# A graph layer on one core: one turn's rows fetched by SP, a longer reach for the gathers, early statistics moved into the turns

## The reference

```
h   = relu(layernorm(x))                          # nodes
xn  = silu(h @ aw1 + ab1) @ aw2 + ab2             # the table, one row per node
W   = silu(edge_attr @ fw1 + fb1) @ fw2 + fb2     # filters, one row per edge, 50 inputs
agg = segment_sum(W * xn[src], dst)               # message of each edge, summed by node
out = x + h + silu(agg @ ow1 + ob1) @ ow2 + ob2
```

## Time and profile before

| | us |
|---|---|
| runs | 2394.49, 2394.53, 2397.10 (median 2394.53) |
| profiled execution, its own time | 2395.59 |
| its span in the trace | 2393.7 |
| PE busy / VectorE busy / ACT busy / POOL busy | 1300.2 / 1178.2 / 520.4 / 1525.4 |
| mean granted clock of TensorE | 0.74 of full speed |

### The profile page before, as it was taken

One profiled execution on the slowest core, in us unless ns is written; L12 is line 12 of the kernel. 1 busy time (PEld: TensorE's weight loads), 2 busy tenths in 40 slices (PEclk: granted clock), 3 DMA queues, 4 the chain that ended last, 5 costly groups with the idle time before them and its releaser, 6 DMA issues.

```text
span 2393.7 us, 13107 instructions
## 1 busy us (share of the span) xinstructions
PE 1300.2 (54%) x4526; PEld 701.8 (29%) x4526; DVE 1178.2 (49%) x1404; ACT 520.4 (22%) x545; POOL 1525.4 (64%) x1619
## 2 busy tenths in 40 slices
PE   2425665656554655566556555655655454555545
PEld 1313332323332333233223222323332232232323
DVE  3635454545554554555535544644454453554545
ACT  2312222212221222222222211211222121121211
POOL 7246666666666666666666666666666666666664
PEclk8667776778777677777668777876778686776776
DMA  4312122212212222212212212212212212212211
GB/s 140 143 30 79 45 80 81 75 54 84 82 51 81 53 75 79 81 47 82 86 45 83 80 46 88 79 50 84 83 51 80 81 50 81 80 51 85 56 46 37
DMA packets 62292, 171.46 MB, mean 72 GB/s; under 512 B 27088, under 2 KB 29648, under 8 KB 59024
## 3 DMA queue, kind: packets, MB, share of 16 engines
q0 software_dynamic: 51584, 105.75, 17.1%
q1 hardware_dynamic: 8192, 61.32, 6.8%
q10 hardware_dynamic: 2448, 3.54, 0.4%
HBM read 164.08 MB, written 6.42 MB: 71 GB/s over the span
## 4 chain that ended last, share of the span: by engine, by line
another core or an unknown queue 40%; PE 27%; ACT 15%; issue 14%; DVE 3%; DMA 0%; ACTq 0%; SPq 0%; DVEq 0%
PE banks L872 15%; ACT hid L435 7%; PE banks L864 7%; ACT hid L441 7%; PE banks L879 3%; PE banks L887 1%; PE banks L811 1%; ACT hs L455 1%; DVE stats L643 0%; ACT mid L464 0%; DVE stats L544 0%; PE banks L806 0%; PE banks L818 0%; DMA xs<-in_x 0%
## 5 line engine op out<-in xcount | busy, mean ns | idle before, releaser
L369 POOL DMA_INDIRECT xg<-node_table,src x1564 | 1478.6, 945 | 828.3 <-issue 453.2
L872 PE MATMUL banks<-hid,wts 128*128 128x512 f32 x806 | 535.3, 799 | 565.4 <-ACT hid L435 436.6
L672 DVE TENSOR_TENSOR banks<-banks,xg 128x1024 f32<-128x1024 f32 (+1 forms) x198 | 241.0, 1217 | 1090.2 <-remote 899.2
L864 PE MATMUL banks<-attr,wts 50*128 50x512 f32 x806 | 293.9, 810 | 444.8 <-issue 250.4
L675 DVE TENSOR_REDUCE sums<-banks 128x128 f32<-128x1024 f32 (+1 forms) x408 | 493.9, 1211 | 13.6
L441 ACT ACTIVATE hid<-banks,cols 128x1024 f32<-128x1024 f32 x202 | 224.5, 1111 | 914.0 <-remote 425.7
L435 ACT ACTIVATE hid<-banks,cols 128x1024 f32<-128x1024 f32 x202 | 224.4, 1111 | 825.0 <-remote 595.9
L872 PEld LDWEIGHTS banks<-hid,wts 128*128 128x128 f32 x806 | 179.9, 248 | 755.3 <-ACT hid L435 467.6
L879 PEld LDWEIGHTS banks<-ident,hid 128*128 128x128 f32 x1612 | 225.5, 171 | 204.2 <-issue 198.2
L879 PE MATMUL banks<-ident,hid 128*128 128x128 f32 x1612 | 284.5, 333 | 0.0
L679 DVE TENSOR_TENSOR banks<-banks,other 128x1024 f32<-128x1024 f32 (+1 forms) x204 | 248.7, 1219 | 7.0
(11 more groups left out here) (89 smaller groups left out, 279.5 us busy)
## 6 DMA issues: line engine op xcount, KB each, us to landing
attr<-in_attr SPq DMA_DIRECT2D x25, 2048.0 KB
xg<-node_table,src POOLq DMA_INDIRECT x1564, 2.5
out<-res ACTq DMA_DIRECT2D x8, 256.0 KB
xs<-in_x SPq DMA_DIRECT2D x3, 512.0 KB, 6.0
node_table<-res SPq DMA_DIRECT2D x3, 512.0 KB, 2.8
out<-res ACTq DMA_DIRECT2D x5, 192.0 KB
spare<-in_dst SPq DMA_DIRECT2D x1, 808.0 KB
src<-in_src SPq DMA_DIRECT2D x1, 808.0 KB
```

Of the source, the lines that this page charges most:

```text
L369: pool.indirect_dma_start(xg[:, i % XG, j, :], None, table[:, :], bass.IndirectOffsetOnAxis(ap=src[:, s * L + j:s * L + j + 1], axis=0))\
L672: dve.tensor_tensor(to, to, rows_of, ALU.mult).then_inc(signal, 1)
L864: i = pe.matmul(hid_ps[:, GC * half:GC * half + GC], fw1_s[at, :], attr[at, cols_of], start=True, stop=True)
L872: i = pe.matmul(hid_ps[:, at], w["fw2_s"][:, :], hid[:, s % 2, at], start=True, stop=True)
```

## The change

1. **Early gathers of x wait.** POOL's early gathers for pairs 2, 3, 4 and 5 wait for progress of the node stage (s_tr of chunk 0, then s_res of chunks 0, 1 and 3).
2. **Statistics move into the turns.** bn_stats for early pair r is done by VectorE in turn r + 1, the moments in turn 7, the square root (ACT) in turn 8, the scales in turn 9. Early tasks begin at turn 10, and the early turns become 30, 50, 72, 92, 114 and 136.
3. **fb2** is split only in the slow branch; its scratch now lies in hT.
4. **One turn by SP.** Turn 190 is not gathered by POOL. SP reads each of its 1,024 indices into a register and issues one 512-byte DMA from the table for it, 47 rows after each attr transfer, from turn 8 on, over 22 parts. VectorE waits for four new semaphores in turn 190.
5. **Reach.** POOL waits for fil_done of turn s - 3 instead of s - 2.
6. **Who waits for the gather.** PE waits for it ahead of the transposes, and VectorE no longer does (except in the last two turns). PE's pair sums come ahead of the transposes instead of after the filters, again except in the last two turns.
7. **One-hots** are built per turn with two instructions, in six buffers, instead of per two turns with three.
8. At the end ACT's last "middle" task comes ahead of the "stored" tasks that are left.

```
@@ constants
-BATCH = 2
-OH_SETS = 3
+OH_SETS = 6
-EARLY_TURNS = (20, 40, 64, 84, 108, 128)
-MAIN_TURNS = [s for s in range(PAIRS) if s not in EARLY_TURNS]
+EARLY_TURNS = (30, 50, 72, 92, 114, 136)
+SINGLE_TURN = 190
+MAIN_TURNS = [s for s in range(PAIRS) if s not in EARLY_TURNS and s != SINGLE_TURN]
+SINGLE_PARTS = SINGLE_TURN // PART - 1
+SINGLE_ROWS = -(-PC // SINGLE_PARTS)
+REACH = XG - LAG
+STAT_TURNS = tuple(range(1, EARLY_PAIRS + 1))
+VAR_TURN, STD_TURN, SCALE_TURN, EARLY_FROM = 7, 8, 9, 10
@@ SP
+            def fetch(r):
+                p, j = r // L, r % L
+                t = SINGLE_TURN * L + j
+                node = sp.value_load(src[p:p + 1, t:t + 1], min_val=0, max_val=NODE_TILES * P - 1)
+                sp.dma_start(x_single[p:p + 1, j, :], table[bass.ds(node, 1), :]).then_inc(fetched[r % 4], 16)
             for s in range(PAIRS):
                 pair(s)
+                if s % PART == 0 and s // PART in range(1, SINGLE_PARTS + 1):
+                    if s == PART:
+                        sp.wait_ge(src_in, 16)
+                        sp.wait_ge(s_tab, 16 * (AHEAD + table_writes(N_CHUNKS - 1)))
+                    first = (s // PART - 1) * SINGLE_ROWS
+                    for r in range(first, min(first + SINGLE_ROWS, PC)):
+                        fetch(r)
@@ POOL
+            table_at = {2: (s_tr, 0), 3: (s_res, 0), 4: (s_res, 1), 5: (s_res, 3)}
             for t in range(EARLY_PAIRS * L):
+                if t % L == 0 and t // L in table_at:
+                    signal, c = table_at[t // L]
+                    pool.wait_ge(signal, run(c))
...
-                    pool.wait_ge(fil_done, run(s - 2))
+                    pool.wait_ge(fil_done, run(s - REACH))
@@ ACT
-            act.wait_ge(s_var, 3)
-            act.activation(e_moments[:, 2, :], e_moments[:, 2, :], ACT.Sqrt).then_inc(s_std, 1)
...
+                if s == STD_TURN:
+                    act.wait_ge(s_var, 3)
+                    act.activation(e_moments[:, 2, :], e_moments[:, 2, :], ACT.Sqrt).then_inc(s_std, 1)
@@ VectorE, ahead of the turns (the eight fb2 steps go to the slow branch)
-            for t in range(EARLY_PAIRS * L):
-                if t % L == 0:
-                    dve.wait_ge(e_gathered[t // L], 16 * L)
-                i = dve.bn_stats(stats[:, t, :], e_x[:, t, :])
-            i.then_inc(s_step, 1)
-            step[0] += 1
-            dve.wait_ge(s_step, step[0])
-            moments_of(stats[:, 0:EARLY_PAIRS * L, :], e_moments)
-            scales_of(e_moments, 3)
+            def early_stats(r):
+                dve.wait_ge(e_gathered[r], 16 * L)
+                for t in range(r * L, (r + 1) * L):
+                    i = dve.bn_stats(stats[:, t, :], e_x[:, t, :])
...
@@ VectorE, one-hots
+            def one_hots(s):
+                nodes, to = iota[:, 0:WIN], onehot[:, s % OH_SETS, :, :]
+                dve.tensor_scalar(to[:, 0, :], nodes, ends[:, 0, s:s + 1], None, ALU.is_equal).then_inc(oh_done, 1)
+                dve.wait_ge(oh_done, 2 * s + 1)
+                dve.scalar_tensor_tensor(out=to[:, 1, :], in0=nodes, scalar=ends[:, 1, s:s + 1], in1=to[:, 0, :],
+                                         op0=ALU.is_equal, op1=ALU.subtract).then_inc(oh_done, 1)
@@ VectorE, pair
+                elif s == SINGLE_TURN:
+                    rows_of = x_single[:, :, :]
+                    for signal in fetched:
+                        dve.wait_ge(signal, 16 * PC // len(fetched))
                 else:
                     i = MAIN_OF[s]
                     rows_of = xg[:, i % XG, :, :]
-                    dve.wait_ge(gathered[i % XG], (i // XG + 1) * 16 * L)
...
+                if s in STAT_TURNS:
+                    early_stats(STAT_TURNS.index(s))
+                elif s == VAR_TURN:
+                    dve.wait_ge(s_step, step[0])
+                    moments_of(stats[:, 0:EARLY_PAIRS * L, :], e_moments)
+                elif s == SCALE_TURN:
+                    scales_of(e_moments, 3)
@@ PE, pair
                 pe.wait_ge(red_done, run(s, LAG))
+                if s not in HALVED:
+                    for a in SUMS_AT.get(s, ()):
+                        pair_sums(a)
+                if s in MAIN_OF and s not in HALVED:
+                    pe.wait_ge(gathered[MAIN_OF[s] % XG], (MAIN_OF[s] // XG + 1) * 16 * L)
                 by_edge(s)
                 if s + 1 < PAIRS:
                     filters(s + 1)
-                for a in SUMS_AT.get(s, ()):
-                    pair_sums(a)
+                if s in HALVED:
+                    for a in SUMS_AT.get(s, ()):
+                        pair_sums(a)
```

More of the change, by code:

```diff
@@ L107, in tasks @@
 def tasks():
-    done, free, outs, halves = [], 0, list(range(len(OUTS) - 1)), list(range(2 * EARLY_PAIRS))
+    done, free, outs, halves = [], EARLY_FROM, list(range(len(OUTS) - 1)), list(range(2 * EARLY_PAIRS))
     for s in range(PAIRS):
@@ L279, in gnn_layer @@
         half_gathered = [sem(f"half_gathered{i}") for i in range(2 * len(HALVED))]
+        fetched = [sem(f"fetched{i}") for i in range(4)]
         e_gathered = [sem(f"e_gathered{r}") for r in range(EARLY_PAIRS)]
@@ L452, in task @@
                         act.wait_ge(n_tr, n - 1)
+                    if n == 0:
+                        act.wait_ge(s_rstd, 3)
                     for j in range(TPG):
@@ L473, in _ @@
             act.wait_ge(s_left, 1)
-            act.wait_ge(s_rstd, 3)
             turns(pair, task)
+            task("out", "middle", len(TASKS), len(OUTS) - 1)
             for left in STEPS.get(PAIRS, ()):
                 task(*left)
-            for step in ("middle", "stored"):
-                task("out", step, len(TASKS), len(OUTS) - 1)
+            task("out", "stored", len(TASKS), len(OUTS) - 1)
             n = edges_left(act)
@@ L654, in _ @@
             dve.wait_ge(s_tab, 16 * (AHEAD + table_writes(N_CHUNKS - 1)))
-            def one_hots(k):
-                first, n = k * BATCH, min(BATCH, PAIRS - k * BATCH)
-                nodes = iota[:, 0:WIN].rearrange("p (o w) -> p o w", o=1).to_broadcast([P, n, WIN])
-                for m in range(2):
-                    of_row = ends[:, m, first:first + n].rearrange("p (n o) -> p n o", o=1).to_broadcast([P, n, WIN])
-                    dve.tensor_tensor(onehot[:, k % OH_SETS, 0:n, m, :], nodes, of_row, ALU.is_equal).then_inc(oh_done, 1)
-                dve.wait_ge(oh_done, 3 * k + 2)
-                dve.tensor_tensor(onehot[:, k % OH_SETS, 0:n, 1, :], onehot[:, k % OH_SETS, 0:n, 1, :], onehot[:, k % OH_SETS, 0:n, 0, :],
-                                  ALU.subtract).then_inc(oh_done, 1)
+            def one_hots(s):
[4 more added lines that the diff above has]
+                                         op0=ALU.is_equal, op1=ALU.subtract).then_inc(oh_done, 1)
             def by_tile(s, h, n):
@@ L765, in _ @@
                     dve.wait_ge(s_out[i], 16 * len(OUTS[i::2]))
+                dve.tensor_copy(fb2_part[:, 0, :], rows[:, 0, :]).then_inc(s_fb2, 1)
+                dve.wait_ge(s_fb2, 1)
+                dve.tensor_tensor(fb2_rest[:, 0, :], rows[:, 0, :], fb2_part[:, 0, :], ALU.subtract).then_inc(s_fb2, 1)
+                dve.wait_ge(s_fb2, 2)
+                dve.tensor_copy(fb2_part[:, 1, :], fb2_rest[:, 0, :]).then_inc(s_fb2, 1)
+                dve.wait_ge(s_fb2, 3)
+                dve.tensor_tensor(fb2_rest[:, 1, :], fb2_rest[:, 0, :], fb2_part[:, 1, :], ALU.subtract).then_inc(s_fb2, 1)
+                dve.wait_ge(s_fb2, 4)
+                dve.tensor_copy(fb2_part[:, 2, :], fb2_rest[:, 1, :]).then_inc(s_fb2, 1)
+                dve.wait_ge(s_fb2, 5)
+                dve.wait_ge(s_set, 1)
+                for i in range(3):
+                    dve.tensor_copy(fb2_rows[32 * i:32 * i + 1, :, :],
+                                    fb2_part[32 * i:32 * i + 1, i:i + 1, :].to_broadcast([1, TPG, F])).then_inc(s_fb2, 1)
                 dve.sem_inc(r_msg, 1)
@@ L886, in add_up @@
                 for m in range(2):
-                    i = pe.matmul(sum_ps[:, to:to + WIN], sums[:, at, m, :], onehot[:, s // BATCH % OH_SETS, s % BATCH, m, :],
+                    i = pe.matmul(sum_ps[:, to:to + WIN], sums[:, at, m, :], onehot[:, s % OH_SETS, m, :],
                                   start=False, stop=stop and m == 1)
```

30 lines of the change are left out of this document (10 added, 20 removed).

## The result

| | us |
|---|---|
| kernel before, median (range), 4 runs | 2394.51 (2391.80 to 2397.10) |
| changed kernel, median (range), 4 runs | 2575.47 (2565.87 to 2586.66) |
| ratio, 95% interval | 1.0758 [1.0712, 1.0803] |
| profiled execution of the changed kernel, its own time / span | 2577.17 / 2575.4 |
| mean granted clock of TensorE | 0.719 |

The change made the kernel slower by 7.6%; 2312 us had been forecast, with 2205 to 2392 as the range. It is the way of rival 4: SP paces the kernel.

A forecast was written before the change was run, and what follows sets the result against it. No engine was full; PE's signals came up to 18 us late beside POOL's gathers, with the path in PE and ACT's loop. 2395.6 - 49 (start) - 9 (turn) - 24 (reach) = 2313.6, 1 less for the median: 2312 us, range 2205 to 2392.

The forecast's parts named there:

- rival 4: SP's queue: rows costing over 1.9 us delay attr and pace the kernel; over 2500 us at 2.2 us; chance 4%.
- SP's rows: SP's queue: 47 rows per eight turns at some 1.3 us take 61 of 91 us, so they cost nothing.
- The Trainium skill's price: SP's register load: floor about 600 ns; a row estimated at 1.4 us, a part at 67 us, still covered.
- The rule of the shared port: VectorE's statistics beside POOL's gathers: by the rule up to 13.6 us lost; forecast took nothing, since the trace disagreed.
- The start, 49 us (bounds 31 to 62): Node stage and first turns: earlier table and statistics moved into turns let gather 5 start at 135 instead of 183.96.
- with 17 us to spare for lateness: First turns: fil_done of turn 2 due at about 118, POOL's first five gathers ending at 135.
- One turn less on POOL, 9 us: POOL's gathers: skipping one turn's eight gathers saves 9 us, bounds 2 and 11.4.
- Reach, 24 us between 73 and nothing: POOL's waits for fil_done: waiting three turns back instead of two saves 24 us, a third of 73.
- Rival 2: POOL's waits for fil_done: the reach gives nothing, 2337 us; inside the forecast's range, with which it holds 58%.
- Rival 1: POOL's waits: the reach covers all lateness, saving 246 us instead of 24, so 2092 us; chance 12%.
- rival 3: PE's wait for its gather ahead of by_edge makes turns longer; 2471 us at 0.7 us a turn; chance 8%.
- SP's rows at 1.2 to 1.5 us with idle time before each attr: SP's queue in the changed profile: a sign named as what would show the forecast right.

The follow-up runs named there:

- e13: The changed kernel, unaltered, on a chip where the kernel before takes about 2037 us: 2023.16 us, ratio 0.9931 to the kernel before.
- e16: The changed kernel with turn 190 gathered by POOL again and no rows on SP, chip of 2400: 2372.11 us, ratio 0.9900 to the kernel before.
- e15: The changed kernel with turn 190 gathered by POOL again and no rows on SP, chip of 2037: 2032.71 us, ratio 0.9982 to the kernel before.
- e3: The kernel before plus only the reach, PE's wait for its gather and pair sums ahead of the transposes, chip of 2037: 2037.96 us, ratio 0.9990.
- e10: The kernel before plus only the reach, PE's gather wait and the earlier pair sums, sent again, chip of 2037: ratio 0.9991.
- e18: The kernel before plus only the reach, PE's gather wait and the earlier pair sums, chip of 2400: 2392.59 us, ratio 0.9987.
- e6: The changed kernel with attr's loads from part 2 on issued by ACT instead of SP, chip of 2400: 2558.41 us, ratio 1.0623 to the kernel before.

## Why the prediction was wrong, point by point

**SP's rows: this is the step that failed.** The prediction put it as "with gaps some 1.3 us: 61 us of the 91 that eight turns take. ... Cost nothing; the cover is 30 us per part." A row undisturbed costs 1.24 us, so that was the price of a row on its own, and it held where e13 ran. On the chip that was forecast for, the mean was 2.21 us and a part took 104 us from attr to attr, so the cover of 30 us was not there and the term was not nothing. The price came from one instruction of each kind, at 2254.4 to 2255.1 us, and one sample can't show a tail. A hint of one stood in other rows: for waits named "issue" of many us on PE and VectorE, as the 9.53 us ahead of the moments, the profile names nothing that the engine waited for. I read them as part of the late signals and asked only what they did to PE, ACT and VectorE, not what they would do to SP with six new instructions in each of 1,024 rows. That these waits and SP's long instructions have one cause is not shown; both stand only beside POOL's gathers. Rival 4 had the mechanism, the place, the threshold of 1.9 us and the size right (2.2 us a row, "over 2500"); its 4% rested on the sentence "Nothing in rows 8 comes near it".

**The Trainium skill's price** for a register load (DMA: Bandwidth & Descriptors, "Latency and other measured facts"), about 600 ns, would have made no difference: the median was 495 ns here and 498 in e13. It is given as a floor, and both medians lie under it, so here the measurement decides; and no floor tells what a queue of them costs.

**The rule of the shared port** (SBUF — State Buffer, "SBUF: two separate sides"): the gathers beside the statistics were not held in the changed kernel either (0.94 to 1.01 us each from 90.25 to 250 us), as the prediction had it. The same section says that PE, ACT and VectorE's own ports never wait on anyone. That is said of SBUF's ports and may well hold for them; PE's signals and SP's moves were late all the same, so it is not to be read as "GpSimd can't disturb them".

**The start, 49 us (bounds 31 to 62): mis-sized.** 29 us at gather 5 (183.96 - 154.60), 25 at turn 8 in the changed kernel and 30 in e16, 24 at the end of e16, in which the reach has a share. The step "with 17 us to spare for lateness" failed: ACT stood 31 us for one signal.

**One turn less on POOL, 9 us:** 9.6 us where POOL sets the pace (e15 and e13). On a chip of 2400 no run has it alone.

**Reach, 24 us between 73 and nothing:** 0.1% on chips of 2037 (e3, e10), 3 us by the ratio and 8 by the medians on a chip of 2400, not distinct from nothing (e18, interval 0.9962 to 1.0012). Rival 2 was right about the reach. The turns 8 to 188 took 11.11 us each before, 11.14 in e16 and 11.08 in e18 ((2213.7 - 218.6) / 180 for the last).

**Rival 1** (POOL never waits again, 2092) did not come about on a chip of 2400; **rival 3** did not either: without the rows the turns are as long as before. Of the signs that the prediction named, "SP's rows at 1.2 to 1.5 us with idle time before each attr" is what e13 shows and the changed kernel of the result does not.

**Which version is best?** On chips of 2037 the changed kernel (0.993); on chips of 2400 the one without rows (0.990), which is also faster than before on the others (0.998). Half a turn on SP is never clearly slower (0.996 and 0.998). If a kernel has to run on chips of both kinds, the version without rows is the one to take.

## What to carry to other kernels

A queue that gets a thousand small instructions is an engine to be priced like any other: by the distribution of its instructions in the busiest stretch, not by one clean sample, and against the transfers queued behind them. Here the margin of 30 us a part looked ample and was used up by a tail. Where a trace shows waits that nothing explains ("issue" of many us, "remote" on one core), a change that adds instructions to any sequencer should be priced once with and once without them. Moving the starved transfer to another queue does not help if the rows themselves end too late (e6).

## What the runs showed of the hardware

- The same kernel takes 2394 to 2407 us (medians) in the result and in two groups, and 2035 to 2040 us in the three others. On chips of 2037 no wait in any of the eleven traces is named "remote", and POOL is on 74% of the chain of e13.
- On chips of 2400, while POOL issues gathers, ACT stood up to 31 us for a signal of PE whose matmuls had ended 29 us before ("remote"), and it came when POOL had stopped; SP's instructions came in steps of about 0.70 us, and none of the long moves began with POOL at rest. A row on SP took a mean of 1.27 us with POOL at rest and 2.74 us once POOL had issued for over 11 us. What is behind it (the gathers' descriptors, their traffic, the fetching of SP's 6,000 further instructions, the chip) was not tried.
- So a comparison of two kernels can turn its sign from chip to chip: the changed kernel is 1.0758 times the kernel before on one, 0.9931 times on another.
